# A transformer block with a mixture of experts on one core: routing's last steps, the pads, and the first expert pairs in another order

## The chip, the cores and the metric

The kernel runs on one core of a Trainium2 chip. The time is the device time of the whole program in microseconds; the lower, the better. TensorE is called PE, VectorE DVE, ScalarE ACT, GpSimd POOL and SyncE SP, as in the profile.

## The reference, cut to what matters

```python
x = L0_attn_x                                  # (16, 256, 128): 16 batches of 256 tokens, width 128
x = x + attention(layernorm(x))                # softmax, 16 heads
x = x + recurrence(layernorm(x))               # gated recurrence over 32 steps, its output tanh(...)
x = x + linear_attention(layernorm(x))         # rope, elu + 1 features, 16 heads
x = x + experts(layernorm(x))

def experts(xt):                               # xt: 4096 tokens of 128
    probs = softmax(xt @ Wr + br)              # 16 experts
    w, idx = top_k(probs, 2);  w = w / sum(w)
    h = gelu(xt @ W1[e] + b1[e])               # 128 -> 256, of each expert
    o = h @ W2[e] + b2[e]                      # 256 -> 128
    return xt + sum over the two chosen e of w[e] * o[e]
```

All data are float32. The residual of the last line is over the normalized tokens. Of two experts with logits l0 >= l1 the weights are 1/(1 + exp(l1 - l0)) and exp(l1 - l0)/(1 + exp(l1 - l0)), so one difference and one exponential give both.

## The kernel before, in words

Three parts follow each other. The first (attention and the recurrence, until about 326 us) is not touched.

**Routing.** `linear_attention_and_routing` works through 16 batches of 256 tokens as a pipeline. Each engine has its own function `iteration(n, r)` that lists, in an order written out by hand, the steps of that engine; each step works on batch `b = n - lag` and is left out when `active(n, lag)` is false. The order of the lines is the order of the engine's queue; engines meet only at semaphores (`wait_ge`, `then_inc`). A batch passes through these steps:

- PE and ACT make the recurrence's output, DVE adds it to X (x2), and takes the statistics of the third layernorm (`stats3`, then `mv`). POOL raises the variances of layernorm 3 and 4 to the power -0.5 (`root_power`, two instructions), DVE refines them in four small steps (`root_step` 0 to 3).
- ACT normalizes (`xn3`), PE turns it, makes q, k, v. DVE applies the rotation: t1, two products into t2 (lines 1211 and 1274), and their sum `rot` (line 1137, 128 x 512 with both inputs in SBUF). ACT copies V into `KVones`, makes the exponential and the relu, DVE joins them to `feat`.
- PE, ACT and DVE make the linear attention with its denominator (`KVm`, `den`, `on3`), and DVE adds the result to X (x3, line 1173) and takes `stats4`.
- ACT writes the normalized tokens twice into `pay`, PE makes the logits, ACT copies them. DVE finds the two best (`max`, `max_index`), marks them (`hot`, `sel`), PE counts how many tokens of each expert stand before each token, and DVE makes the place (`place`, `nup`, `mine`, line 1141, `pos`, line 1156). For the weights POOL takes the difference of the two best logits (`gap`, line 1067), ACT its exponential (`odds`, line 1298), DVE `z`, its reciprocal and the weights in `pay`.
- POOL scatters the rows of `pay` to `disp` in DRAM by `pos`: four indirect DMAs a batch (line 1035: two halves of the batch, two choices). Each expert has a region of 4096 + 128 rows there. POOL also adds the token to X (the residual, line 1074) and raises the row numbers in `pay` (the ids, line 1080).

POOL's order in an iteration is: second scatter of the last batch, root, third scatter, gap, fourth scatter, residual, ids, and the first scatter of the next.

**Routing's end.** `plan_tiles` on DVE turns the 16 counts in 17 dependent small steps into a table of 80 tiles of 128 rows (`tablei`): the expert of each tile, and its place in `disp`. `fill_pads` writes 128 empty rows behind the last row of each expert, so that the last tile of an expert reads zeros; SP does it for experts 0 to 7, ACT for 8 to 15. For each it loads the end from `endi` and issues one DMA. It starts after the plan's first step (`endi`).

**Experts.** The 80 tiles are worked on in 40 pairs. SP first waits for the scatters, the weights, the table and all pads, and then issues for each pair one word's load and two DMAs of 128 rows. PE turns the rows (`p_x`), ACT copies them (`xT`), PE multiplies with W1 (eight matmul instructions into `p_hid`), ACT does gelu (four instructions), PE multiplies with W2 (`p_y`), DVE scales by the weight and POOL scatters the rows to `back` (line 1576, two indirect DMAs a pair, 80 in all). DVE copies the weights of each pair's experts ahead (line 1628). In a step PE works on pair i (turn), i-1 (hidden) and i-2 (outputs), in that order; ACT first copies pair i, then does the gelu of pair i-1. At the end SP reads `back`, DVE adds it to X, and SP writes the output.

The lines that the argument about SP rests on are these:

```python
for e in range(q * E // 2, (q + 1) * E // 2):
    end = eng.value_load(endi[0:1, e:e + 1], min_val=e * REGION, max_val=e * REGION + TOKENS)
    eng.dma_start(disp[bass.ds(end, P), :], w["fill"][:, :]).then_inc(pads[q].sem, 16)
...
sp.wait_ge(table.sem, 1)
for q in range(2):
    sp.wait_ge(pads[q].sem, pads[q].at(0))
```

## Time and profile before

| what | us |
|---|---|
| median of three runs | 645.11 (643.07 to 648.98) |
| the profiled execution | 644.1 |
| its span | 642.3 |
| routing's even part in the span | 371.18 to 468.68 |
| first and last scatter of the experts, start | 517.80, 620.83 |

| engine | busy us | share of the span | instructions |
|---|---|---|---|
| PE | 486.8 | 76% | 4082 |
| DVE | 429.6 | 67% | 1260 |
| POOL | 388.7 | 61% | 691 |
| ACT | 341.4 | 53% | 733 |

The shares are means over stages with different limits, so none of them says what bounds the time. The profile follows the chain that ended last back from the end; in the span's last quarter it runs over POOL's scatters to `back`, before them over SP's queue with the pads, and before these over DVE and POOL of the routing. All times in this document that are positions are microseconds from the span's start.

### The profile page before, as it was taken

To read this page: it belongs to the slowest core of one execution; us is meant where nothing else is said; L and a number is where in the kernel's file an instruction comes from. 1 tells how busy PE (TensorE), PEld (TensorE's weight loads), DVE (VectorE), ACT (ScalarE), POOL (GpSimd) and SP (SyncE) were. 2 spreads that over 40 slices of the span, in tenths; PEclk is the share of its full clock that TensorE was granted. 3 is DMA by queue.
4 is the path that set the end of the run, shared out by engine and by line. 5 is a ranking of instruction groups with operands and counts; after the bars stand their busy time and mean duration, and the time that the engine had idled before them with its cause. 6 is when DMAs were issued, how large, how long until landed. Compare 5 with 4: busy or idle time off the path is not lost. (4 is left out here: it accounts for less than half of the span.)

```text
span 642.3 us, 14722 instructions
## 1 busy us (share of the span) xinstructions
PE 486.8 (76%) x4082; PEld 323.2 (50%) x4082; DVE 429.6 (67%) x1260; ACT 341.4 (53%) x733; POOL 388.7 (61%) x691
## 2 busy tenths in 40 slices
PE   1368899999999999988667887776861199899900
PEld 0123455555555555544434565454541199888800
DVE  6376778888888888852238889888866356555306
ACT  2016667777777777667215666655532076565600
POOL 4564587777777776332341477777777057777750
PEclk9999999999999999999859989999755599999955
DMA  2577444443443343200053000010012333333219
GB/s 65 139 181 188 105 101 122 101 103 103 101 100 101 98 109 102 55 4 2 0 168 101 13 31 31 30 35 30 31 35 65 71 98 95 97 95 100 77 53 350
DMA packets 66417, 55.97 MB, mean 87 GB/s; under 512 B 8477, under 2 KB 59826, under 8 KB 66354
## 3 DMA queue, kind: packets, MB, share of 16 engines
q1 hardware_dynamic: 58466, 45.12, 27.0%
q0 software_dynamic: 4608, 8.47, 4.0%
q10 hardware_dynamic: 3280, 1.65, 1.0%
q8 instruction: 27, 0.44, 0.3%
q14 instruction: 36, 0.29, 0.2%
HBM read 30.53 MB, written 25.71 MB: 88 GB/s over the span
## 5 line engine op out<-in xcount | busy, mean ns | idle before, releaser
L419 DVE TENSOR_REDUCE negmax<-p_dve 128x4 f32<-128x1024 f32 x128 | 155.8, 1220 | 44.3 <-PE p_dve L622 42.5
L518 ACT ACTIVATE probs<-p_exp 128x1024 f32<-128x1024 f32 x128 | 130.7, 1021 | 31.2 <-PE p_exp L596 30.7
L1576 POOL DMA_INDIRECT back<-XN2T,rows x80 | 79.9, 999 | 43.2 <-DVE XN2T L1636 21.9
L1035 POOL DMA_INDIRECT disp<-pay,pos x64 | 65.4, 1021 | 31.2 <-DVE pos L1156 19.4
L613 PE MATMUL p_out<-probs,V 128*32 128x256 f32 x1024 | 69.9, 391 | 0.0
L622 PE MATMUL p_dve<-KS,QS 61*128 61x256 bf16 x512 | 52.9, 289 | 13.6 <-DVE negmax L419 12.0
L1662 ACT ACTIVATE hid<-p_qkv,own 128x128 f32<-128x128 f32 x160 | 45.6, 368 | 24.6 <-PE p_qkv L1689 20.3
L596 PE MATMUL p_exp<-QS,KS 64*128 64x256 bf16 x512 | 51.0, 278 | 8.5 <-ACT probs L518 4.5
L1689 PE MATMUL p_qkv<-XN2T,own 128*128 128x128 f32 x320 | 44.2, 282 | 0.0
L1628 DVE COPY own<-expert 128x514 f32 x80 | 35.6, 446 | 12.7 <-issue 12.7
L1689 PEld LDWEIGHTS p_qkv<-XN2T,own 128*128 128x128 f32 x320 | 39.9, 196 | 0.9
L613 PEld LDWEIGHTS p_out<-probs,V 128*32 128x32 f32 x1024 | 27.1, 110 | 25.3 <-issue 14.3
L67 POOL TENSOR_SCALAR root<-mv 128x2 f32<-128x2 f32 x32 | 7.1, 221 | 51.4 <-DVE mv L411 50.2
L622 PEld LDWEIGHTS p_dve<-KS,QS 61*128 61x128 bf16 x512 | 22.8, 98 | 28.6 <-DVE negmax L419 23.9
L596 PEld LDWEIGHTS p_exp<-QS,KS 64*128 64x128 bf16 x512 | 14.7, 94 | 35.6 <-issue 15.5
L651 PE MATMUL p_misc<-ident,xn 128*128 128x128 f32 x64 | 15.2, 323 | 21.0 <-POOL xn L325 20.4
L570 ACT ACTIVATE gate<-p_misc,gates_bh 128x256 f32<-128x256 f32 x32 | 13.4, 470 | 23.1 <-PE p_misc L718 23.1
L69 POOL TENSOR_TENSOR root<-root,power 128x2 f32<-128x2 f32 x32 | 22.9, 717 | 2.7
L651 PEld LDWEIGHTS p_misc<-ident,xn 128*128 128x128 f32 x64 | 6.9, 150 | 34.4 <-POOL xn L325 19.2
L323 POOL TENSOR_TENSOR xn<-X,mv 128x256 f32<-128x256 f32 x32 | 19.6, 613 | 5.2 <-POOL root L78 2.1
L717 PE MATMUL p_misc<-xn2T,gates_w 128*128 128x256 f32 x64 | 20.8, 407 | 2.4 <-DVE carry L431 0.8
L675 PE MATMUL p_misc<-xn1T,Wqk 128*128 128x256 f32 x64 | 21.9, 473 | 1.0 <-ACT xn1T L529 0.9
(246 smaller groups left out, 1224.8 us busy)
## 6 DMA issues: line engine op xcount, KB each, us to landing
scratch<-part SPq DMA_DIRECT2D x32, 192.0 KB, 2.1
KS<-scratch SPq DMA_DIRECT2D x32, 192.0 KB, 3.3
QS<-scratch SPq DMA_DIRECT2D x32, 192.0 KB, 4.4
rows<-disp SPq DMA_DIRECT2D x80, 65.0 KB
scratch<-part SPq DMA_DIRECT2D x32, 128.0 KB, 1.9
own<-back SPq DMA_DIRECT2D x8, 512.0 KB, 6.4
expert<-in_W_dram SPq DMA_DIRECT2D x1, 2064.0 KB, 8.9
scratch<-part SPq DMA_DIRECT2D x32, 64.0 KB, 1.9
```

The source lines that it names most:

```text
L69: pool.tensor_tensor(y, v, t["power"][:, 0:TT], ALU.pow).then_inc(mark.sem, 1)
L419: dve.tensor_reduce(negmax[q][:, i, :, 2 * hp:2 * hp + 2], p_dve[buf][:, :].rearrange("p (v w k) -> p v w k", v=HALF, k=S), AX.X, ALU.max, ...
L518: act.activation(probs[s % 4][:, :, :, :].rearrange("p v w q -> p (v w q)"), p_exp[:, :], ACT.Exp)\
L596: mm = pe.matmul(p_exp[:, (2 * v + w) * S:(2 * v + w + 1) * S], KS[q][rows, h, kt * P:(kt + 1) * P], QS[q][rows, h, :], start=True, stop=True)
L613: mm = pe.matmul(p_out[32 * j:32 * j + 32, 0:S], values[:, first:first + 32], probs[s % 4][:, j % HALF, j // HALF, :], start=(s % 4 == 0), ...
L622: mm = pe.matmul(p_dve[buf][:, (2 * v + w) * S:(2 * v + w + 1) * S], QS[q][rows, h, i * P:(i + 1) * P], KS[q][rows, h, :], start=True, sto ...
L651: mm = pe.transpose(dst[:, i * P:(i + 1) * P], src[:, i, :], ident[:, :])
L1035: pool.indirect_dma_start(out=disp, out_offset=bass.IndirectOffsetOnAxis(ap=pos[q][:, i, k:k + 1], axis=0), in_=pay[q][:, k, i, :], in_off ...
L1576: pool.indirect_dma_start(out=back, out_offset=bass.IndirectOffsetOnAxis(ap=rows[r][:, h, D + 1:ROW].bitcast(U32), axis=0), in_=y[r][:, h, :],
L1628: dve.tensor_copy(own[r][:, h, :], w["expert"][:, bass.ds(es[h], 1), :].rearrange("p o c -> p (o c)")).then_inc(w_s.sem, 1)
L1662: act.activation(hid[q][:, h, c, :], p_hid[q % 2][:, (2 * h + c) * P:(2 * h + c + 1) * P], ACT.Gelu, bias=own[q][:, h, HID + c:HID + c + 1 ...
L1689: mm = pe.matmul(p_hid[q % 2][:, (2 * h + c) * P:(2 * h + c + 1) * P], own[q][:, h, c * P:(c + 1) * P], xT[q][:, h * P:(h + 1) * P], start ...
```

## The change

**Two pad ends in a word.** The counts, without the region's start, are packed in pairs, the second shifted by 13 bits, with three more plan steps for one less (17 become 19). SP takes the pairs of experts 0-1, 4-5, 8-9, 12-13, ACT the others; each loads four words instead of eight and issues eight DMAs as before. The pads start after the plan's fourth step. **A tile for every expert:** an expert without rows gets one tile (the clamp to P). **First pads with their own signal:** the pads of experts 0 to 3 count on `pads_first`; SP waits for these before it starts, and for the other twelve only before pair 2.

```diff
-            then(dve.tensor_copy(endi[:, :], count[:, :]))
+            then(dve.tensor_tensor(full[:, :], count[:, :], w["region"][:, :], ALU.subtract))
+            then(dve.tensor_copy(endi[:, :], full[:, :]))
+            ends = endi[:, :].rearrange("p (j k) -> p j k", k=2)
+            then(dve.tensor_scalar(ends[:, :, 1], ends[:, :, 1], END_BITS, None, ALU.logical_shift_left))
+            then(dve.tensor_tensor(ends[:, :, 0], ends[:, :, 0], ends[:, :, 1], ALU.bitwise_or))
...
-            then(dve.tensor_tensor(full[:, :], count[:, :], w["region"][:, :], ALU.subtract))
-            then(dve.tensor_scalar(counti[:, :], full[:, :], float(P - 1), None, ALU.add))
+            then(dve.tensor_scalar(counti[:, :], full[:, :], float(P - 1), float(P), ALU.add, ALU.max))
...
-            eng.wait_ge(plan.sem, plan.at(0, 1))
+            eng.wait_ge(plan.sem, plan.at(0, 4))
             eng.wait_ge(fill_set.sem, fill_set.at(0))
-            for e in range(q * E // 2, (q + 1) * E // 2):
-                end = eng.value_load(endi[0:1, e:e + 1], min_val=e * REGION, max_val=e * REGION + TOKENS)
-                eng.dma_start(disp[bass.ds(end, P), :], w["fill"][:, :]).then_inc(pads[q].sem, 16)
+            for pair in range(q, E // 2, 2):
+                word = eng.value_load(endi[0:1, 2 * pair:2 * pair + 1], min_val=0, max_val=(TOKENS << END_BITS) + TOKENS)
+                for k in range(2):
+                    rows = nc.s_assert_within((word >> END_BITS * k) & ((1 << END_BITS) - 1), 0, TOKENS,
...
+                    place = rows + (2 * pair + k) * REGION
+                    eng.dma_start(disp[bass.ds(place, P), :], w["fill"][:, :])\
+                        .then_inc(pads_first.sem if pair < FIRST_PADS // 2 else pads[q].sem, 16)
...
+        sp.wait_ge(pads_first.sem, pads_first.at(0))
         sp.wait_ge(table.sem, 1)
-        for q in range(2):
-            sp.wait_ge(pads[q].sem, pads[q].at(0))
...
+            if isinstance(i, int) and 2 * i == FIRST_PADS:
+                for q in range(2):
+                    sp.wait_ge(pads[q].sem, pads[q].at(0))
```

**The routing's order.** Blocks that stood at the start of DVE's, PE's and POOL's iteration stand at its end, with the lag lowered by one, so that the pipelines are one iteration shorter; ACT's logits copy goes the other way. Apart from this rotation, these instructions change places in their engine's cyclic order:

- DVE before: t1, x2, t2 (line 1211), KVm, root 0, 1, 2, max, root 3, max_index, den, hot, reciprocal, sel, z, on3, t2 (line 1274), place, reciprocal of z, nup, rot, mine, pay, pos, stats3, x3, feat, stats4.
- DVE after: x2, t1, t2, KVm, root 0, **second t2**, root 1, max, **root 2**, max_index, den, **root 3**, hot, reciprocal, sel, z, on3, **reciprocal of z**, place, **rot, nup, stats3**, mine, pay, pos, x3, feat, stats4.
- POOL before: first scatter, second, root, third, gap, fourth, residual of this batch, ids of the next. POOL after: residual of this batch, its ids, first scatter, root, second, third, fourth scatter; no gap.
- ACT: V's copy goes from behind on3T to between the logits' copy and the exponential.
- PE: only rotated.

**The logits' difference by ACT.** The exponential takes it as scale and bias, one instruction for each half of the batch:

```diff
-                    pool.tensor_tensor(gap[:, :], best[:, :, 1], best[:, :, 0], ALU.subtract).then_inc(gap_s.sem, 1)
...
-                    act.wait_ge(gap_s.sem, gap_s.at(b))
+                    act.wait_ge(top_s.sem, top_s.at(b, TT))
...
-                    act.activation(odds[:, 1, :], gap[:, :], ACT.Exp).then_inc(odds_s.sem, 1)
+                    for i in range(TT):
+                        act.activation(odds[:, 1, i:i + 1], best[:, i, 0:1], ACT.Exp, bias=best[:, i, 1:2], scale=-1.0).then_inc(odds_s.sem, 1)
```

**The first pairs.** With FILL = 3, PE and ACT do the older pairs first in the steps 0 to 3; from step 4 on the order is as before:

```diff
+        def step(i, k, r):
+            if isinstance(i, int) and i <= FILL:
+                hidden(i, k, r)
+                outputs(i, k, r)
+                turn(i, k, r)
+            else:
+                turn(i, k, r)
+                hidden(i, k, r)
+                outputs(i, k, r)
```

ACT likewise: `hidden` (gelu) and then `turned` (the copy) up to step 3, `turned` and then `hidden` after it.

## Rows read from the trace of the kernel before

**Rows 1.** Stage table, routing's even part: us, busy (instructions) of each engine, clock, DMA.

```profile
371.18:468.68 97.50, 74.09 (x430) 51.46 (x431) 85.49 (x413) 55.49 (x149) 75.20 (x99) 0.94 0.10 31
```

**Rows 2.** Timeline of POOL over one routing period: start us, duration us, engine, line, operation.

```profile
417.87 0.96 POOL L1035 DMA_INDIRECT disp<-pay,pos  x1 [0.30 <-DVE stats L1189]
...
419.18 1.04 POOL L1053 TENSOR_TENSOR root<-root,power 128x4 f32<-128x4 f32 x1
420.42 1.09 POOL L1035 DMA_INDIRECT disp<-pay,pos  x1 [0.20 <-issue]
421.54 0.21 POOL L1067 TENSOR_TENSOR gap<-best 128x2 f32<-128x2 f32 x1
421.90 0.99 POOL L1035 DMA_INDIRECT disp<-pay,pos  x1 [0.16 <-issue]
422.91 0.70 POOL L1074 TENSOR_TENSOR X<-X,pay 128x256 f32<-128x256 f32 x1
423.70 0.57 POOL L1080 TENSOR_SCALAR pay<-pay 128x4 int32<-128x4 int32 x1
425.37 1.07 POOL L1035 DMA_INDIRECT disp<-pay,pos  x1 [1.10 <-DVE pos L1156]
```

**Rows 3.** Timeline of DVE in the same period; brackets: idle before, and its releaser.

```profile
420.25 0.16 DVE L1104 TENSOR_TENSOR root<-root 128x4 f32<-128x4 f32 x1 [0.66 <-POOL root L1053]
...
423.00 1.17 DVE L1137 TENSOR_TENSOR rot<-t 128x512 f32<-128x512 f32 x1
...
424.34 0.22 DVE L1156 TENSOR_REDUCE pos<-mine 128x4 uint32<-128x64 f32 x1
424.48 0.48 DVE L1162 BATCH_NORM_STATS2 stats<-X 128x6 f32<-128x128 f32 x2
...
425.25 0.39 DVE L1173 TENSOR_TENSOR X<-p_u,X 128x256 f32<-128x256 f32 x1
```

**Rows 4.** One line's instructions (rot on DVE): duration ns min/median/max, first and last start.

```profile
L1137 DVE TENSOR_TENSOR rot<-t x16: 681/1171/1180, 338.8 to 467.3; 128x512 f32<-128x512 f32 x16
```

**Rows 5.** One line's instructions (the pads' DMAs on SP): duration ns, first and last start.

```profile
L958 SPq DMA_DIRECT2D disp<-fill x8: 332/332/372, 493.5 to 501.5; - x8
```

**Rows 6.** The chain of waits from the last pad to the first rows: start us, us.

```profile
501.51 4.14 DMA disp<-fill
...
506.62 0.37 SPq L1600
...
507.36 0.35 SPq L1600
...
508.56 0.34 SPq L1600
```

**Rows 7.** Timeline of PE and ACT at the first expert pairs.

```profile
509.31 0.66 PE L1679 MATMUL p_ta<-ident,rows 128*128 128x128 f32 x2 [12.98 <-DMA rows<-disp]
510.01 0.38 ACT L1654 ACTIVATE XN2T<-p_ta 128x256 f32<-128x256 f32 x1 [18.15 <-PE p_ta L1679]
...
512.04 1.91 PE L1689 MATMUL p_qkv<-XN2T,own 128*128 128x128 f32 x8
...
513.99 1.14 ACT L1662 ACTIVATE hid<-p_qkv,own 128x128 f32<-128x128 f32 x4 [1.32 <-PE p_qkv L1689]
514.17 1.18 PE L1689 MATMUL p_qkv<-XN2T,own 128*128 128x128 f32 x8
```

**Rows 8.** Timeline of POOL, first and last scatter of the expert stage.

```profile
517.80 1.01 POOL L1576 DMA_INDIRECT back<-XN2T,rows  x1 [19.12 <-DVE XN2T L1636]
...
620.83 0.97 POOL L1576 DMA_INDIRECT back<-XN2T,rows  x1 [0.30 <-issue]
```

**Rows 9.** Timeline of ACT in the same period.

```profile
421.77 0.20 ACT L1298 ACTIVATE odds<-gap 128x2 f32<-128x2 f32 x1 [2.27 <-POOL gap L1067]
```

**Rows 10.** Timeline of POOL near routing's end: first scatter right after the ids.

```profile
486.25 1.07 POOL L1035 DMA_INDIRECT disp<-pay,pos  x1 [0.78 <-POOL pay L1080]
```

**Rows 11.** Timeline of DVE in the tile plan, four steps merged.

```profile
493.38 0.81 DVE L927 TENSOR_TENSOR tiles<-tiles 128x16 f32<-128x16 f32 x4
```

More of the change, by code:

```diff
@@ new lines, in iteration @@
+                if active(n, 5):
+                    b = n - 5
+                    dve.wait_ge(pos_s.sem, pos_s.at(b, 3))
+                    if b >= PAIR:
+                        dve.wait_ge(sent[b % PAIR].sem, sent[b % PAIR].at(b // PAIR - 1))
+                    with nc.allow_low_precision(reason="one term of each sum is not zero, and it is a whole number"):
+                        dve.tensor_reduce(pos[o][:, :, :], mine[:, :, :, :], AX.X, ALU.add).then_inc(pos_s.sem, 1)
+                if active(n, 3):
+                    b = n - 3
+                    dve.wait_ge(u_p.sem, u_p.at(b))
+                    dve.wait_ge(nm3.sem, nm3.at(b))
+                    dve.tensor_tensor(X[:, bass.ds(2 * b, 2), :], p_u[:, 0:S].rearrange("p (i d) -> p i d", i=TT), X[:, bass.ds(2 * b, 2), :], ALU.add)\
+                        .then_inc(x3_s.sem, 1)
@@ L1286, in _ @@
+            pipeline(dve, iteration, 5)
             plan_tiles(dve)
@@ L1670, in expert_pe, with turn @@
         pe.wait_ge(table.sem, 1)
-        def step(i, k, r):
+        def turn(i, k, r):
             if i is not None:
```

296 lines of the change are left out of this document (146 added, 150 removed).

## The prediction

> **What bounds the kernel now.** I read the stage table first, then one period of the routing stage engine by engine, then the chain of waits from the last batch to the first expert pair, and last the scatters of the expert stage.
>
> In the routing stage each batch takes one period. The window of [rows 1] is 97.50 us long and holds 99 POOL instructions; a period has nine (four scatters, two of the root, gap, residual, ids), so these are eleven periods of 8.86 us. No engine is full: DVE is busy 85.49 of 97.50. What sets the period is a loop over two engines. DVE writes pos, which ends at 424.56; POOL starts the first scatter at 425.37, 0.8 us later, then comes a second, then the root ([rows 2] show the second scatter and the root of the period before, 417.87 to 420.22); DVE has nothing left to do for 0.66 us until the root is there ([rows 3]) and takes 4.31 us from it to the end of the next pos (420.25 to 424.56). POOL's part is 8.86 - 4.31 = 4.55 us. A second thing to see: POOL's residual (422.91, 0.70 us) and DVE's rot (423.00) overlap, and rot takes 1.17 us, where its shortest takes 0.681 ([rows 4]).
>
> Between the routing and the experts nobody computes. After the last pos SP and ACT issue eight pads each, 1.14 us apart ([rows 5]); SP waits 4.14 us for the last, and only then issues the first rows ([rows 6]). PE turns them at 509.31, and the first scatter of the experts starts at 517.80 ([rows 7, 8]). From there POOL issues 80 scatters without a hole to 620.83: 103.03 / 79 = 1.30 us each, 2.6 per pair of tiles. POOL bounds that stage, so the end of the kernel moves with the first of these scatters, 517.80, and with nothing else of the stage's middle.
>
> **The rotation costs nothing.** Most of the diff moves the blocks across the iteration's start with the lag lowered by one. The instructions of one engine then come in the same cyclic order, with the same waits; PE is only rotated. What is left are these real moves.
>
> **Routing, per period.** (a) POOL's second scatter (0.96 us, and 0.30 before it) goes behind the root. After the end of pos = 0: first scatter 0.8 to 1.9, root to 3.3 ([rows 2]: 418.83 to 420.22 is 1.39), and DVE goes on at 3.3, no longer at 4.55. (b) DVE's stats of X now stand before mine and pos: + 0.77 (424.48 to 425.25, [rows 3]) between root and pos. (c) The third rotation product is brought between the root's steps: the work is the same, it fills short gaps; I count 0, at most 0.2. (d) Gap leaves POOL: 0.21 and the slots around it, 421.51 to 421.90, are replaced by the 0.30 that stands between two scatters, so 0.1 us. ACT does two exps of 0.20 us for one, and the copy of V stands in front of them; it idles 2.27 us before the exp ([rows 9]), and V's copy is 0.38 (the same size as the one of [rows 7]). Cost 0; if that cover were gone, DVE's z would wait up to 0.4 us. (e) The residual and the ids stand ahead of the batch's own scatters instead of behind the last batch's: the same place in the cycle, right after a fourth scatter.
>
> If rot kept its 1.17 us the loop would be 3.3 + 4.31 + 0.77 = 8.4. But where does the residual fall now? POOL from pos = 0: root to 3.3, 0.20, scatter 1.09, 0.30, 0.96, 0.30, 0.96, so the residual runs from 7.1 to 7.8. Rot starts at 3.3 + 2.75 = 6.05 (420.25 to 423.00), ahead of it: 0.49 less. Mine comes 0.68 + 0.77 later, at 7.5, inside the residual: it pays instead, between 0 and 0.70, and I take rot's own 0.49. So the stall is handed on, not removed. The loop is 8.4 - 0.49 + 0.49 = 8.4 with both, 7.9 with neither. Followed from the residual's end instead, mine, pay and pos need some 0.4 more, which gives 7.8 + 0.4 = 8.2; I take that.
>
> The next bound stands close behind: POOL's own queue. 1.07, 1.39, 0.20, 1.09, 0.30, 0.96, 0.30, 0.96, 0.03, 0.70, 0.09, ids 0.23 to 0.57, and 0.78 from ids to the next scatter ([rows 10]) give 8.1 to 8.4. So the new period is 8.2, with bounds 8.0 and 8.5: 0.66 us less than 8.86. I count 12 periods (eleven of the window and one for the uneven ones at its ends): 7.9 us. Once, the first batch's pos comes 0.77 later behind the stats: less 0.8. In the tail the root can stand in POOL's queue waiting for its stats with a scatter behind it; nothing to at most 0.7, I take 0.1. Routing: **-7.0 us**, bounds -3.5 and -9.5.
>
> The Trainium skill, SBUF: State Buffer, section Who interferes with whom, says that a DVE instruction with two SBUF inputs and a GpSimd instruction that reads SBUF lock each other out for the whole instruction, whoever starts first. By that rule rot and mine each wait for the residual's end; the trace agrees for rot, which ends 0.56 us after the residual does.
>
> **From the last pos to the first expert scatter.** Two more plan steps and the pads four steps in instead of one: a step is 0.2 us (0.81 for four, [rows 11]), so the pads start 0.6 later, at 494.1 instead of 493.5. The table is 0.4 later and waits for nobody: 17 + 2 steps of 0.2 and the short ones behind them are done while the pads go out. A word now gives two DMAs. The rows' loads of SP already do this: 506.62, 507.36, 508.56, that is 1.94 a word and 0.74 inside ([rows 6]). Eight pads: 3 x 1.94 + 0.74 = 6.56 instead of 7.98, the last at 500.7 instead of 501.5. SP then no longer waits 4.14, since its remaining waits are over: the first pads went out 6 us earlier, and POOL's last scatter ends 0.8 + 1.07 + 3 x 1.26 = 5.7 after pos and has 4 us more to land, as long as a pad takes. About 0.5 for the issue and the waits, 0.97 from there to the first row DMA (505.65 to 506.62): 502.2, the second 502.9, and PE at + 1.95 (507.36 to 509.31) = 504.9: 4.4 us earlier. The other end: if the reads stand behind the pads in the DMA engines, they start when the last has landed, 500.7 + 4.14 + 1.95 = 506.8, and 2.5 is left. I take 4.2. The wait for all pads before pair 2 ends at 504.9 at the latest, when pair 1 has just been issued: 0. The clamp to one tile an expert adds no instruction, and all 80 tiles were run before.
>
> **Order of the first pairs.** With T = PE's first turn: turn 0.66, copy 0.38, hidden 0 from T+1.15, at 1.91 (the slow clock) to T+3.1 ([rows 7]). Then ACT does the four gelus first (1.14) and the copy of pair 1 behind them, so hidden 1 starts at T+4.65; before it started at T+4.86. From there to the first scatter 3.63 (514.17 to 517.80). That is 0.2 won. But until pair 4 each pair now goes hidden 1.06 to 1.18, gelus 1.14, copy 0.38, with hand-overs about 2.9 us in series, where POOL takes 2.6: it starves 0.3 for each of two or three pairs. And PE, which went from 1.91 to 1.18 for the eight hidden matmuls while it was busy without a hole from 512.04, has a hole of 0.9 us after turn 1; if its clock stays at 1.2 GHz for one or two pairs more, each costs 0.75 and the outputs as much. Bounds: -0.2 and +2.8; I take **+1.1**, between. So the hand-over gains 4.2 - 1.1 = **3.1 us**.
>
> **The sum** is 7.0 + 3.1 = 10.1 us. Against the profiled execution, 644.1 (span 642.3 and 1.8 around it), that is 634.0; its time is 1.0 under the median of the three runs, 645.11, which gives 635.0. I write 634.5, between the two.
>
> **Rivals.** (1) Rot on a scatter, the slower case. Rot now starts at 6.05, where POOL's third scatter (4.9 to 5.85) ends and the fourth begins (6.15). If a scatter shuts out a DVE instruction with two SBUF inputs as the residual does, rot waits for 7.1, and if POOL's residual slips in ahead of it, for 7.8; rot, stats, mine and pos then end at 7.8 + 0.68 + 0.77 + 0.5 = 9.75. Twelve periods of + 0.9 are + 10.8, less the 3.1 gained: 653. It turns slower from a period of 9.1 on. Against it: from 420.42 to 422.89 POOL is in a scatter nearly all the time, and DVE gets through its stretch from root to rot without a hole in it. Chance 0.05. (2) Something else closes the routing loop: rot waits only for the scatter, or DVE for ACT's exps, and the period stays near 8.8. Left are 3.1 and a little: 641. For it: three engines hang on each other within 0.3 us here. 0.18. (3) The first pads' own signal does not do what it says: the reads stand behind the pads and PE starts cold, so the hand-over gains 0 to 1: 637.5. 0.12. (4) Better than forecast: neither rot nor mine meets the residual and POOL's slots close up, period 8.0, and no starving: 630. 0.15.
>
> **Chances.** The forecast (period 8.1 to 8.35 and 2 to 4 us at the hand-over, 632 to 637) has 0.50. A measurement can tell about 1% (6.5 us) from no change: faster means under 638.7. The forecast, case 4 and most of case 3 lie there, with a part of case 2: 0.76; within 1%: 0.19; slower 0.05. The range that leaves out two in ten takes in cases 4 and 2: 629 to 642.
>
> **What will show it.** Routing: first scatters 8.2 us apart (8.87 now); DVE's wait for the root under 0.3; rot at 0.68 and mine at about 0.7; the ACT row before the exp still idle. Hand-over: last pad on SP 6.6 us after the first instead of 8.0; first rows without the 4.14 us wait; PE's first turn 10.8 us after the first pad instead of 15.8; first expert scatter about 9 us after the turn instead of 8.5. From there to the end 124.5 us as before. If the period is over 8.6 the POOL and lock arithmetic is wrong; if the turn comes over 12.5 us after the first pad, the reads queue behind the pads.

## The result and the profile after

| | before, us | after, us |
|---|---|---|
| median of 20 runs each, in turn on one chip | 645.22 (641.59 to 651.56) | 642.75 (636.30 to 650.22) |
| the profiled execution, its span | 644.1, 642.3 | 639.8, 638.0 |

The ratio after to before is 0.9919, 95% interval 0.9893 to 0.9945: 5.2 us faster. It leaves out the slow runs, which are over 1.5% above their kernel's fastest (five of after's 20 and one of before's), while the medians in the table hold all of them and are 2.5 us apart. The forecast was a gain of 10.6. 642.75 lies outside the range of 629 to 642, and nearest to rival 2's 641.

I cut both traces at the same five events: the first scatter of routing's first and of its last batch, PE's first turn of an expert pair, POOL's first expert scatter and its last.

| stretch, us | before | after | change | forecast |
|---|---|---|---|---|
| start to the first batch's scatter | 363.13 | 360.23 | -2.9 | 0 |
| first to last batch | 129.99 | 122.69 | -7.3 | -7.0 |
| last batch to PE's turn | 16.19 | 13.01 | -3.2 | -4.2 |
| turn to the first expert scatter | 8.49 | 10.24 | +1.7 | +1.1 with the next |
| first to last expert scatter | 103.03 | 108.82 | +5.8 | 0 |
| last expert scatter to the end | 21.47 | 23.01 | +1.5 | 0 |

The first row is not the change's: that part of the kernel is the same, and in 19 traces of the two kernels and their variants it was between 359.8 and 368.5, on average 363.1 with the old routing and 362.9 with the new. So this one pair of profiles flatters the change by 3 us there, and the two last rows take 7.3 away.

**Routing.** The stage table of after, over twelve periods from the third batch to the fifteenth (columns as in [rows 1]), has 97 POOL instructions in 99.11 us, eight a period instead of nine, and 8.26 us a period:

```profile
376.53:475.64 99.11, 74.50 (x428) 52.02 (x428) 83.76 (x421) 59.60 (x159) 77.01 (x97) 0.86 0.10 34
```

The timeline of POOL in one period of after (against [rows 2]):

```profile
389.99 0.96 POOL L1046 DMA_INDIRECT disp<-pay,pos  x1 [0.30 <-issue]
390.98 0.69 POOL L1072 TENSOR_TENSOR X<-X,pay 128x256 f32<-128x256 f32 x1
391.76 0.23 POOL L1078 TENSOR_SCALAR pay<-pay 128x4 int32<-128x4 int32 x1
392.76 1.07 POOL L1046 DMA_INDIRECT disp<-pay,pos  x1 [0.77 <-POOL pay L1078]
393.86 0.24 POOL L1062 TENSOR_SCALAR root<-mv 128x4 f32<-128x4 f32 x1
394.18 1.04 POOL L1064 TENSOR_TENSOR root<-root,power 128x4 f32<-128x4 f32 x1
```

The period is 8.12 here, and what stands before the first scatter is no longer DVE's pos but POOL's own ids, as in [rows 10]: in an undisturbed period POOL's queue is the bound. The timelines of DVE and ACT of the same period (against [rows 3, 4, 9]):

```profile
387.13 0.16 DVE L1109 TENSOR_TENSOR root<-root 128x4 f32<-128x4 f32 x1 [0.27 <-POOL root L1064]
...
389.37 0.68 DVE L1228 TENSOR_TENSOR rot<-t 128x512 f32<-128x512 f32 x1
...
390.83 0.27 DVE L1246 TENSOR_TENSOR mine<-hot,place 128x64 f32<-128x64 f32 x1
391.02 0.68 DVE L1253 TENSOR_TENSOR pay<-odds,z 128x4 f32<-128x4 f32 x1
391.62 0.21 DVE L1261 TENSOR_REDUCE pos<-mine 128x4 uint32<-128x64 f32 x1
```

```profile
387.71 0.39 ACT L1312 ACTIVATE KVones<-p_qkv 128x256 f32<-128x256 f32 x1 [0.53 <-DVE t L1158]
387.99 0.47 ACT L1320 ACTIVATE odds<-best 128x1 f32<-128x1 f32 x2
```

DVE's wait for the root is 0.27 (0.66 before), rot takes 0.68, and the residual (390.98 to 391.67) is paid for by the instruction behind mine, the weights in `pay`: 0.68 us for an operation on 128 x 4 that usually took 0.15 in before, ending as the residual ends. The stall was handed on, to a neighbour of the one I named. ACT's 2.27 us of idleness before the exp, which I expected to stay, are gone, filled by V's copy and the second exp, and DVE's z waits for neither.

**The hand-over.** SP's pads, the chain from the last scatter, and the landing time of routing's scatters in a usual period (the last column):

```profile
484.03 6.58 SPq L968 DMA_DIRECT2D disp<-fill  x8
```

```profile
485.55 0.96 POOL disp L1046
486.51 0.30 issue
486.81 5.71 DMA disp<-pay,pos
492.60 0.27 SPq L1601
...
493.36 0.37 SPq L1608
494.08 1.71 DMA rows<-disp
```

```profile
disp<-pay,pos POOLq DMA_INDIRECT x4, 2.3
```

The eight pads take 6.58 us for the forecast 6.56. The chain no longer has a pad in it: it runs over the last scatter's landing, which takes 5.71 us from the scatter's start, where 2.3 is usual in the routing. But the last scatter of before, which also runs beside the 16 pads, is late too:

```profile
disp<-pay,pos POOLq DMA_INDIRECT x1, 5.0
```

It landed at 502.0, hidden behind the last pad, which landed at 505.65 ([rows 6]). In e1 to e7 the last landing takes 4.4 to 5.1 us. So the change didn't bring the late landing, it uncovered it.

**The first pairs.** PE and ACT (against [rows 7]):

```profile
495.93 0.66 PE L1697 MATMUL p_ta<-ident,rows 128*128 128x128 f32 x2 [9.32 <-DMA rows<-disp]
497.06 2.07 PE L1709 MATMUL p_qkv<-XN2T,own 128*128 128x128 f32 x8 [0.47 <-ACT XN2T L1662]
499.17 1.14 ACT L1672 ACTIVATE hid<-p_qkv,own 128x128 f32<-128x128 f32 x4 [2.16 <-PE p_qkv L1709]
...
500.64 2.07 PE L1709 MATMUL p_qkv<-XN2T,own 128*128 128x128 f32 x8 [1.08 <-ACT XN2T L1662]
...
505.75 2.07 PE L1709 MATMUL p_qkv<-XN2T,own 128*128 128x128 f32 x8 [0.47 <-ACT XN2T L1662]
...
510.41 1.16 PE L1709 MATMUL p_qkv<-XN2T,own 128*128 128x128 f32 x8 [0.26 <-ACT XN2T L1662]
```

Three pairs' hidden matmuls take 2.07, where before only the first was slow (1.91). PE stands before each of them, and its granted clock stays at 1.2 GHz until 509.3, for 13.4 us after the first turn; before it was 5.1. And POOL:

```profile
511.00 0.98 POOL L1582 DMA_INDIRECT back<-XN2T,rows  x1 [2.54 <-DVE XN2T L1644]
...
513.96 0.98 POOL L1582 DMA_INDIRECT back<-XN2T,rows  x1 [0.70 <-issue]
```

It starves 2.24 and 0.40 us beyond its usual 0.30.

**The middle of the experts.** The expert scatters of before and of after, each as a row of the lines by form (busy us, mean ns, idle us before them):

```profile
L1576 POOL DMA_INDIRECT back<-XN2T,rows x80 | 79.9, 999 | 43.2 <-DVE XN2T L1636 21.9 <-issue 21.3
```

```profile
L1582 POOL DMA_INDIRECT back<-XN2T,rows x80 | 83.1, 1039 | 45.1 <-DVE XN2T L1644 23.1 <-issue 22.0
```

The same 80 scatters take 3.2 us more, and that is all of the difference from the fifth to the last (97.85 and 101.03 us). Three of before are over 1.2 us, 14 of after; over 1.1 us are 7 and 19. Most others are at 0.97 or 0.98. DVE, then POOL, around two of the long ones of after:

```profile
517.50 0.51 DVE L1636 COPY own<-expert 128x514 f32 x1
...
518.03 0.41 DVE L1636 COPY own<-expert 128x514 f32 x1
```

```profile
516.52 1.23 POOL L1582 DMA_INDIRECT back<-XN2T,rows  x1 [0.30 <-issue]
518.06 1.23 POOL L1582 DMA_INDIRECT back<-XN2T,rows  x1 [0.30 <-issue]
```

A copy of an expert's weights (518.03) starts 0.03 before the scatter (518.06) and ends 0.38 into it; all 14 of over 1.2 us look so. The copy before it, which began while a scatter ran, is itself 0.51 instead of 0.42. The same trace holds a test of whether any DVE instruction would do this, an addition with one input in PSUM, and a hit by a copy that is nearer its end:

```profile
533.21 0.42 DVE L1644 TENSOR_TENSOR XN2T<-p_r,rows 128x256 f32<-128x256 f32 x1 [1.20 <-PE p_r L1724]
533.26 0.98 POOL L1582 DMA_INDIRECT back<-XN2T,rows  x1 [0.30 <-issue]
...
571.14 0.43 DVE L1636 COPY own<-expert 128x514 f32 x1 [0.52 <-issue]
571.33 1.09 POOL L1582 DMA_INDIRECT back<-XN2T,rows  x1 [0.30 <-issue]
```

The addition stands as the copy does, and the scatter stays at 0.98. The copy at 571.14 has 0.24 us left when the scatter starts, and costs 0.11. Over all nine traces with plain copies the same sum holds: where a copy began over 0.03 us before a scatter and had over 0.13 us left, in 147 cases, the scatter is longer by what was left of the copy less 0.13 us, to within 0.06; the additions that stood across a start, 89 of them, left it at 1.03 or less. The Trainium skill (SBUF — State Buffer, section Who interferes with whom) says that a copy in its fast mode and GpSimd block each other for a whole instruction, and that writing the descriptors of a GpSimd DMA needs the shared port. The traces agree, and price it: up to 0.25 us a hit.

### The profile page after: what moved, and what is told of

Same layout as the page of the kernel before. It is cut to its first block and busy times, and to the rows that moved or that the text cites. A ratio compares the mean times of both kernels' runs of the same rounds, so it can differ in the third digit from the quotient of the medians.

```text
span 638.0 us, 14709 instructions
## 1 busy us (share of the span) xinstructions
PE 487.8 (76%) x4082; PEld 324.2 (51%) x4082; DVE 428.4 (67%) x1262; ACT 348.1 (55%) x749; POOL 386.5 (61%) x675
## 5 line engine op out<-in xcount | busy, mean ns | idle before, releaser
L1582 POOL DMA_INDIRECT back<-XN2T,rows x80 | 83.1, 1039 | 45.1 <-DVE XN2T L1644 23.1
L1046 POOL DMA_INDIRECT disp<-pay,pos x64 | 66.1, 1032 | 30.8 <-issue 13.1
L613 PE MATMUL p_out<-probs,V 128*32 128x256 f32 x1024 | 68.5, 385 | 0.0
L1709 PE MATMUL p_qkv<-XN2T,own 128*128 128x128 f32 x320 | 46.6, 291 | 2.3 <-ACT XN2T L1662 2.3
L1709 PEld LDWEIGHTS p_qkv<-XN2T,own 128*128 128x128 f32 x320 | 41.2, 202 | 4.8 <-ACT XN2T L1662 3.7
L596 PEld LDWEIGHTS p_exp<-QS,KS 64*128 64x128 bf16 x512 | 14.7, 94 | 35.5 <-issue 15.5
L570 ACT ACTIVATE gate<-p_misc,gates_bh 128x256 f32<-128x256 f32 x32 | 13.4, 471 | 23.3 <-PE p_misc L718 23.3
L1363 ACT ACTIVATE pay<-X,root 128x256 f32<-128x256 f32 x32 | 17.4, 593 | 14.2 <-issue 12.0
```

Of the source, the lines that this page charges most:

```text
L596: mm = pe.matmul(p_exp[:, (2 * v + w) * S:(2 * v + w + 1) * S], KS[q][rows, h, kt * P:(kt + 1) * P], QS[q][rows, h, :], start=True, stop=True)
L613: mm = pe.matmul(p_out[32 * j:32 * j + 32, 0:S], values[:, first:first + 32], probs[s % 4][:, j % HALF, j // HALF, :], start=(s % 4 == 0), ...
L1046: pool.indirect_dma_start(out=disp, out_offset=bass.IndirectOffsetOnAxis(ap=pos[q][:, i, k:k + 1], axis=0), in_=pay[q][:, k, i, :], in_off ...
L1582: pool.indirect_dma_start(out=back, out_offset=bass.IndirectOffsetOnAxis(ap=rows[r][:, h, D + 1:ROW].bitcast(U32), axis=0), in_=y[r][:, h, :],
L1709: mm = pe.matmul(p_hid[q % 2][:, (2 * h + c) * P:(2 * h + c + 1) * P], own[q][:, h, c * P:(c + 1) * P], xT[q][:, h * P:(h + 1) * P], start ...
```

## The experiments

The theory after the first look: routing pays as forecast, the hand-over pays less because of the last scatter's landing, and the rest is lost at two places where the forecast saw none: the order of the first pairs under the slow clock, and copies that lengthen the scatters of a stage bound by POOL. The rival: the order is harmless and the whole shortfall lies in the routing, or comes with the pads. Every kernel was run in five rounds in turn with the kernel before, six or twelve times. All times below are from profiled executions; "fifth to last" is from POOL's fifth expert scatter to its last.

| kernel | ratio to before (95%) | routing, first to last batch | last batch to turn | turn to fifth scatter | fifth to last | scatters busy |
|---|---|---|---|---|---|---|
| before | 1 | 129.99 | 16.19 | 13.67 | 97.85 | 79.9 |
| after | 0.9919 (0.9893, 0.9945) | 122.69 | 13.01 | 18.03 | 101.03 | 83.1 |
| e1, old order of pairs | 0.9892 (0.9831, 0.9953) | 123.02 | 12.55 | 14.37 | 100.21 | 82.3 |
| e2, only the order | 1.0015 (0.9970, 1.0060) | 129.94 | 15.95 | 16.04 | 98.09 | 80.1 |
| e3, only routing | 0.9905 (0.9865, 0.9946) | 125.69 | 15.60 | 15.43 | 99.86 | 82.0 |
| e4, only routing's end | 0.9965 (0.9925, 1.0005) | 130.64 | 12.90 | 13.49 | 99.22 | 81.2 |
| e5, extra matmuls | 0.9870 (0.9807, 0.9933) | 127.75 | 13.14 | 13.05 | 100.79 | 82.9 |
| e6, the same, old order | 0.9876 (0.9817, 0.9936) | 125.22 | 13.79 | 12.22 | 99.81 | 81.8 |
| e7, copies with two inputs | 0.9956 (0.9916, 0.9995) | 123.35 | 13.12 | 16.34 | 104.48 | 87.1 |

**e1, the old order of the first pairs.**

```diff
-FILL = 3
+FILL = -1
```

> The changed kernel with one part undone: PE and ACT work on the first pairs in the old order (turn, hidden, outputs; copy, gelu). Theory A (the new order leaves PE in holes behind ACT, its clock stays at 1.2 GHz, and POOL starves): the fifth expert scatter starts about 13.7 us after PE's first turn, as before the change, instead of 18.0, and the time falls by about 4 us against the changed kernel, ratio to the kernel before 0.983 to 0.988. Theory B (the expert stage lost its time to DVE's weight copies and POOL's scatters shutting each other out, whatever the order): the fifth scatter may come earlier, but the number of scatters over 1.2 us stays near 20 and the time falls by at most 1 us, ratio about 0.991. Theory C (the gain of the routing is not real in most runs): about 1.00.

Turn to fifth scatter falls from 18.03 to 14.37 us, without a hole before any scatter. PE's timeline of e1, the first three pairs:

```profile
500.13 1.91 PE L1709 MATMUL p_qkv<-XN2T,own 128*128 128x128 f32 x8
...
502.26 1.91 PE L1709 MATMUL p_qkv<-XN2T,own 128*128 128x128 f32 x8
...
506.02 1.06 PE L1709 MATMUL p_qkv<-XN2T,own 128*128 128x128 f32 x8
```

PE runs on without a hole from its second turn, and the clock is up 7.4 us after the first. This is theory A's time to the fifth scatter; the gain by the ratio, 0.9892, is a little smaller than it said (0.983 to 0.988), and its interval covers that of after. Ten scatters are over 1.2 us.

**e2, before with the new order alone** (`step` of PE and ACT as in the change, FILL = 3; nothing else).

```diff
+            if isinstance(i, int) and i <= FILL:
+                hidden(i, k, r)
+                outputs(i, k, r)
+                turn(i, k, r)
```

> The kernel before with the new order of the first pairs alone. Theory A: fifth expert scatter 17 to 18 us after PE's first turn instead of 13.7, 4 us slower, ratio 1.006. Theory B: the first scatter moves by under 2 us and the time by nothing that can be told, unless the scatters over 1.2 us become many more than 5; ratio 0.998 to 1.003.

2.4 us more to the fifth scatter than before (16.04, 13.67), less than theory A's 17 to 18, and a ratio above 1 that can't be told from it. The order costs, with either hand-over.

**e3, before with the routing's part alone**: the moved steps and the difference by ACT; the pads, the plan and the order are those of before.

```diff
-                    act.activation(odds[:, 1, :], gap[:, :], ACT.Exp).then_inc(odds_s.sem, 1)
+                    for i in range(TT):
+                        act.activation(odds[:, 1, i:i + 1], best[:, i, 0:1], ACT.Exp, bias=best[:, i, 1:2], scale=-1.0).then_inc(odds_s.sem, 1)
```

> The kernel before with the routing's part alone (orders of DVE, POOL, ACT and PE, the exponential of the logits' difference by ACT); plan, pads and the order of the first pairs are the old ones. Routing gains what its trace shows: the last batch's first scatter 10 us earlier, hand-over 24.7 us as before, expert stage 103 us. All theories but C: 635, ratio 0.984 to 0.987. Theory C: 0.995 or above. Theory B leaves open 0 to 4 us of longer scatters by chance of phase.

6.1 us by the ratio, with 2.6 either way: the change's gain and perhaps more, but not the 8 to 10 that was expected. The trace has 125.69 us from the first to the last batch, 3 more than after: most periods are 8.1, but four are 8.9 to 9.6. POOL's timeline at one of them, where the first scatter comes 9.60 us after the last batch's:

```profile
408.23 1.06 POOL L1035 DMA_INDIRECT disp<-pay,pos  x1 [1.93 <-ACT pay L1352]
```

This trace also shows that the old order alone doesn't bring the fifth scatter at 13.7. Its clock comes up 8.6 us after the turn, as in e2 with the new order, and its fifth scatter 15.43 us after it. In the eight traces with the old order and no extra matmuls the clock is up 5.1 to 8.6 us after the turn, in the seven with the new 8.6 to 13.4. On the later chips the fifth scatter comes after 15.5 to 16.6 us with the old order and 17.2 to 17.7 with the new.

**e4, before with routing's end alone** (plan, pads, signal; routing and order of before).

```diff
+        sp.wait_ge(pads_first.sem, pads_first.at(0))
         sp.wait_ge(table.sem, 1)
-        for q in range(2):
-            sp.wait_ge(pads[q].sem, pads[q].at(0))
```

> The kernel before with the end's part alone (two pad ends per word, first pads with their own signal, one tile for every expert), old routing order and old order of the first pairs. PE's first turn 3 us earlier after the last batch's first scatter, 13.0 instead of 16.2; the last scatter of the routing lands in about 5.7 us instead of 2.3, which now ends SP's wait. Theories A and B: 642, ratio 0.993 to 0.997. If the pads were hidden behind something else: 1.00.

The turn comes 12.90 us after the last batch's first scatter instead of 16.19, and the fifth scatter 3.5 us earlier; the ratio gives 2.3 us. The last landing takes 4.76 us here, not the 5.7 that I expected. Routing and hand-over together are worth 8.4 by the ratios of e3 and e4, the order costs 1.0 by that of e2: 7.4, where after measures 5.2 with an interval of 3.5 to 6.9. Each of the three is uncertain by 2.6 to 2.9 us, so the two sums can't be told apart.

**e5 and e6, extra matmuls before the first pair**, to raise the clock; e5 with the new order, e6 with the old (FILL = -1). Nothing reads their product.

```diff
         pe.wait_ge(table.sem, 1)
+        for _ in range(13):
+            pe.matmul(p_hid[1][:, 0:256], ident[:, :], w["expert"][:, 0, 0:256], start=True, stop=True)
```

> The changed kernel with 13 extra matmuls of 128x256 on PE (their result is overwritten) in the 8 us in which PE waits for the first rows. If the slow clock is what makes the new order dear, the first hidden matmuls take 1.1 us instead of 2.07, the fifth expert scatter comes 15 us after the first turn instead of 18.0, and about 3 us are gained. If the serial order itself costs it, the clock is at 2.4 GHz and the fifth scatter still comes after 17 us or more. Theory B (shut-outs between DVE's copies and POOL's scatters): nothing from the fifth scatter to the last changes, 99 to 101 us.

> The same extra matmuls, and the old order of the first pairs. The difference to the kernel with the new order and the same clock is the order's own price: theory A says 1.5 to 2 us at the fifth scatter (12.5 to 13 us after the turn). Time about 634, ratio 0.982. Theory B: from the fifth scatter to the last as with the new order.

PE of e5, the first two pairs:

```profile
503.18 1.16 PE L1711 MATMUL p_qkv<-XN2T,own 128*128 128x128 f32 x8 [0.47 <-ACT XN2T L1662]
...
505.84 1.16 PE L1711 MATMUL p_qkv<-XN2T,own 128*128 128x128 f32 x8 [1.06 <-ACT XN2T L1662]
```

The clock is at 2.4 GHz from 4.6 and 2.8 us before the turn. There the new order needs 13.05 us to the fifth scatter and the old 12.22. So the order's own price is 0.8 us (1.5 to 2 was expected), by one trace of each (0.6 by e2 and e3, whose clocks come up together); the rest of its 2.4 us (e2 against before) to 3.7 us (after against e1) is the clock that it keeps down. Both kernels have the lowest ratios of all, and cannot be told apart by them.

**e7 and e8, the weight copies as an instruction with two inputs** (x * 0 + x, both from SBUF), to take them out of the fast mode; e8 with the old order and the extra matmuls. The small copy of b2 is changed likewise, here and in the later kernels.

```diff
-                    dve.tensor_copy(own[r][:, h, :], w["expert"][:, bass.ds(es[h], 1), :].rearrange("p o c -> p (o c)")).then_inc(w_s.sem, 1)
+                    one = w["expert"][:, bass.ds(es[h], 1), :].rearrange("p o c -> p (o c)")
+                    dve.scalar_tensor_tensor(out=own[r][:, h, :], in0=one, scalar=0.0, in1=one, op0=ALU.mult, op1=ALU.add).then_inc(w_s.sem, 1)
```

> The changed kernel, but DVE copies the experts' weights with a two-operand instruction (x * 0 + x, both operands the same tile) instead of its copy. Theory B: such an instruction does not keep POOL from writing descriptors, so no scatter of the expert stage is over 1.2 us, their busy time is 78 instead of 83.1, the stretch from the fifth scatter to the last is 96.3 us instead of 101.0, and the time falls by 4 us or more, ratio 0.984 to 0.987. Theory A: the weight copies are longer and nothing is gained; ratio 0.991 or more.

> All three together: old order of the first pairs, extra matmuls before them, weight copies with two operands. If theories A and B are both right, fifth scatter 13 us after the turn and 96.3 us from it to the last: 9 us less than the changed kernel in the expert stage, about 632, ratio 0.977 to 0.981. If one of them is wrong, that part's 4 us are missing.

The opposite of what I expected. DVE, then POOL, of e7:

```profile
517.11 0.69 DVE L1637 SCALAR_TENSOR_TENSOR own<-expert 128x514 f32 x1
```

```profile
517.21 1.44 POOL L1582 DMA_INDIRECT back<-XN2T,rows  x1 [0.48 <-issue]
```

The scatter that starts under the longer instruction takes 1.44 us, the stage 104.5 instead of 101.0. The instruction had 0.59 us left, so the copy's sum (less 0.13) gives 1.44 here too: this instruction with two inputs in SBUF holds a scatter back as the copy does, and longer because it is longer. In the nine traces of before, after and e1 to e7 the stretch from the fifth scatter to the last is the scatters' busy time and 17.3 to 18.0 us more, so a longer scatter lengthens the stage by as much. e8's ratio is 0.9897 (0.9857, 0.9936), 0.2% above its sister e6, where 0.977 to 0.981 was expected; its profile isn't read.

**e9, e10, e11: the copies as a reduce over one element**, which the Trainium skill's same section lists as never contending on trn2. e9 is after, e10 before, e11 after with the old order and the extra matmuls.

```diff
-                    dve.tensor_copy(own[r][:, h, :], w["expert"][:, bass.ds(es[h], 1), :].rearrange("p o c -> p (o c)")).then_inc(w_s.sem, 1)
+                    one = w["expert"][:, bass.ds(es[h], 1), :].rearrange("p o c -> p c o")
+                    dve.tensor_reduce(own[r][:, h, :], one, AX.X, ALU.max).then_inc(w_s.sem, 1)
```

> The changed kernel with DVE's weight copies as a reduction over an axis of one element (max): one operand in SBUF, about 0.6 us for 514 elements instead of 0.43. The kernel with two operands made the shut-outs worse (scatters up to 1.4 us, 104.5 us from the fifth to the last), so theory B now reads: any DVE instruction that reads SBUF through a second port holds POOL back, the longer the more, and one with a single plain operand does not. It expects all scatters at 0.97 to 1.0, busy time 78, 96 to 97 us from the fifth to the last, 4 us less than the changed kernel, ratio 0.984 to 0.988. The rival: any longer DVE instruction at a scatter's start delays it, and this one does as well: 103 us or more. The Trainium skill, SBUF: State Buffer, Who interferes with whom, says of tensor_reduce on this chip that it never contends.

> The kernel before with the same weight copies. Theory B: the kernel before had few shut-outs (97.9 us from the fifth scatter to the last), so it gains 1.5 us at most, ratio 0.996 to 1.000; with the changed kernel and the same copies beside it the whole of the change then shows, 8 to 9 us. The rival: 103 us, slower by 5.

> The changed kernel with the reduction as copy, the old order of the first pairs and the 13 extra matmuls before them: fifth scatter 12.5 us after the turn, 96 to 97 us from there to the last. Theories A and B together: 9 to 10 us under the changed kernel's expert stage, time about 633, ratio 0.976 to 0.982, under both kernels. If the reduction does not free POOL: 0.985 to 0.99, as with the old order alone.

No scatter is long any more; its row of one line in e9 (ns min/median/max):

```profile
L1582 POOL DMA_INDIRECT back<-XN2T,rows x80: 978/982/997, 511.6 to 648.1; - x80
```

and in e12, DVE's reduce starts 0.10 us before a scatter and has 0.59 left at its start, as the instruction of e7 had, with no effect:

```profile
519.57 0.69 DVE L1637 TENSOR_REDUCE own<-expert 128x514 f32 x1
519.67 0.98 POOL L1582 DMA_INDIRECT back<-XN2T,rows  x1 [0.30 <-DVE XN2T L1646]
```

But the times don't price it. On this chip the kernel before took 678.5 us, and the expert stage of all three kernels has 35 to 36 us of holes before POOL's scatters, 15 or 16 of about 2.2 us and some smaller ones, where before's own trace has none; at more than half of them PE, DVE and ACT have stood together shortly before, for 0.9 to 2.8 us. The ratios are 0.9888 (0.9850, 0.9926), 1.0007 (0.9979, 1.0036) and 0.9906 (0.9872, 0.9940).

**e12 to e17, the same kernels on other chips.** e12 and e16 are e9, e13 and e17 are e10, e14 is e11; e15 is after with reduces and FILL = -1, without the extra matmuls.

> The kernel after with the experts' weight copies done by a reduce over one element, once more, because the chip of the last comparison showed holes of 35 us in the expert stage, in which POOL is not the bound and a longer scatter costs nothing. Theory (copies lengthen the scatters, which bound the stage on an undisturbed chip): no scatter over 1.2 us, and fifth to last scatter 97.5 to 98.5 us where the changed kernel had 101.0; the whole time 2 to 3.5 us under the changed kernel's, a ratio to the kernel before of 0.985 to 0.989. Rival (the longer scatters are filled from slack elsewhere): 101 us again, with holes before the scatters, and a ratio of 0.992.

> The kernel before with the same copies by reduce. Theory: the profiled run of the kernel before had only 2 long scatters and 97.9 us from the fifth to the last, so a profile hardly changes (97.5 to 98.5), but its usual run is likely to have more of them (variants had 7 to 18), so the median falls by 0 to 2 us: ratio 0.997 to 1.000. Rival: ratio 1.000 or above, as the longer DVE instruction (0.69 us for 0.42) costs what the scatters win.

> The kernel after with copies by reduce, the old order of the first pairs and extra matmuls before the first pair. Theory: routing -7.3, hand-over -2.5 to -4, expert stage 97.5 to 98.5: the whole 9 to 11 us under the kernel before, ratio 0.983 to 0.986, the forecast's size. Rival (the longer scatters cost nothing): as its sister with plain copies, 0.9876.

> The kernel after with copies by reduce and the old order of the first pairs, nothing else. Theory, on a chip whose expert stage has no holes: fifth to last scatter 97.5 to 98.5 us, turn to fifth scatter 13.5 to 14.5: 9 to 11 us under the kernel before, ratio 0.983 to 0.986. Rival (longer scatters cost nothing): as the old order with plain copies, 0.9892. On a chip with holes: 0.989 either way.

> The kernel after with copies by reduce, in case this chip has no holes in the expert stage. Theory: 97.5 to 98.5 us from fifth to last scatter, ratio 0.985 to 0.989. Rival: 100 to 101 us and 0.992.

> The kernel before with copies by reduce, in case this chip has no holes in the expert stage. Theory: 97.5 to 98.5 us, ratio 0.997 to 1.000. Rival: 1.000 or above.

| kernel | ratio to before (95%) | before there, us | fifth to last | longest scatter |
|---|---|---|---|---|
| e12 | 0.9921 (0.9878, 0.9964) | 677.5 | 129.83 | 1.00 |
| e13 | 0.9982 (0.9947, 1.0016) | 677.5 | 128.53 | 1.01 |
| e14 | 0.9893 (0.9857, 0.9930) | 677.5 | 129.96 | 1.00 |
| e15 | 0.9884 (0.9845, 0.9923) | 675.6 | 127.11 | 1.00 |
| e16 | 0.9946 (0.9907, 0.9986) | 675.6 | 126.60 | 1.00 |
| e17 | 1.0056 (1.0021, 1.0091) | 675.6 | 128.72 | 1.01 |

The holes again, so no price again. Nine traces of 80 scatters, and not one over 1.01 us.

**e18, the changed kernel unaltered**, on such a chip.

> The changed kernel unaltered, as the control for the nine runs with reduces: in their calls the kernel before took 675 to 678 us, and the reduces' traces have 16 holes of about 2.2 us before POOL's scatters in the expert stage. If the holes are the chip's, this trace has them too (33 to 36 us), with scatters over 1.2 us beside them, and the ratio is 0.989 to 0.993. If they are the reduces', this trace has under 4 us of holes, and the kernel before takes 643 to 648 us.

The ratio is 0.9933 (0.9894, 0.9971), before took 675.9, and the trace has 31 us of holes: they belong to the chips, not to the reduce. POOL's timeline shows one, and a lengthened scatter:

```profile
560.58 0.98 POOL L1582 DMA_INDIRECT back<-XN2T,rows  x1 [2.23 <-DVE XN2T L1644]
...
563.28 1.07 POOL L1582 DMA_INDIRECT back<-XN2T,rows  x1 [0.42 <-issue]
```

With copies, five scatters are over 1.1 us here (19 in after's first trace). What holds the engines up on these chips stays open.

**What the traces show together.** From the first to the last batch, the six traces with the old routing took 129.9 to 131.0 us. The thirteen with the new took 122.7 to 130.0, on average 125.7. The profile of after is the best of the thirteen. The periods say how: from the second batch to the thirteenth they are 8.81 to 8.90 with the old routing, in all six traces, but for the last one in two of them (9.18 and 9.28). With the new they start at 8.08, and in each trace some are held up: one of the eleven is over 8.6 us in after, three in e3, e5 and e6 each, six in e11, the longest 10.53.

What holds them up is a wait that neither the prediction nor the words ahead of it name. ACT writes a batch's tokens into one of two buffers `pay`, and must first wait until the scatters of the batch two before have landed:

```python
if b >= PAIR:
    act.wait_ge(sent[b % PAIR].sem, sent[b % PAIR].at(b // PAIR - 1))
```

One of the longest periods, in e5: the landing time of the scatter at 366.91 (the last of its batch), then ACT and POOL,

```profile
disp<-pay,pos POOLq DMA_INDIRECT x1, 4.2
```

```profile
371.14 1.09 ACT L1363 ACTIVATE pay<-X,root 128x256 f32<-128x256 f32 x2 [2.58 <-issue]
...
379.69 1.15 POOL L1046 DMA_INDIRECT disp<-pay,pos  x1 [2.83 <-ACT pay L1363]
```

The scatter lands at 371.06 and ACT goes on at 371.14; the profile calls the wait "issue", but the landing is what ends it. In the traces that record these landings (not all do), ACT starts `pay` within 0.1 us of one in 49 of 61 batches with the new routing, and in 3 of 33 with the old, where 1.0 us of slack is usual. A landing mostly takes 2.3 us from the scatter's start. With the old routing five took over 3 us (up to 4.34), and the periods behind them are 8.81 to 8.88. With the new nine did: one of 3.23 in after costs nothing (8.15), and behind the other eight stand periods of 8.87 to 10.53. Five periods of over 8.6 in these traces (8.80 to 9.16) come without a late landing. Why some scatters land late isn't known.

The slow clock may add to it. In e3 it is at 1.2 GHz from 402.5 to 405.9, inside the period of 9.60. In e5 it falls only at 378.2, when most of the delay is there. The kernel before takes both at once without a loss. There a scatter lands after 3.54 us, and the clock is slow from 371.1 to 374.5; stage table of 3 us,

```profile
371.00:374.00 3.00, 3.00 (x8) 1.62 (x7) 2.60 (x15) 2.24 (x4) 1.49 (x2) 0.51 0.09 26
```

and the next first scatter comes 8.81 us after the last, as always. How much of a long period is the landing's and how much the clock's, no run separates.

## Why the prediction was wrong, step by step

**The routing's bound: right, its size right only undisturbed.** The loop over DVE and POOL, the root's wait, rot at 0.68, a stall that is handed on and POOL's queue close behind all stand in the trace. POOL's queue gives 8.11, the lower end of 8.1 to 8.4. But I read the regularity of the old period as a property of the work. It was that of its slack: the buffer wait for the landings stands in both kernels, I put it at nothing without looking, and the shorter period uses up the 1.0 us of slack that hid it. The typical gain is 4.6 us over all traces (130.3 to 125.7), and 5.6 (130.2 to 124.6) over those of ordinary chips (where before takes 645 to 648 us), not 7.0; the bounds of -3.5 to -9.5 hold both.

**The hand-over's start: right mechanism, 1.0 us too much.** The pads are as forecast. Their signal works: the turn comes 11.9 us after the first pad, where I forecast 10.8 and named 12.5 as the sign that the reads queue behind the pads. What is off is SP's last wait, which I called over. Pos ended at 492.31 in before, so my own terms (5.7 to the scatter's end, 4 more to land) put the landing at 502.0, and SP was to be through at 501.2: 0.8 us that I dropped. The landing itself came 4.75 us after the scatter's end instead of 4, another 0.75; 0.5 came back in smaller terms. That the pads in flight make it late is likely, since it is 2.3 from the start in the routing, against 5.0 to 5.7 here; no run took the pads away. In this trace the first reads are as quick beside the pads as without them, 2.57 us from the first row DMA to the turn for 2.69 before. In e1, e4, e5, e6 and e7 the landing is earlier and the reads take 3.3 to 4.4, so there they seem to be held up in part, and over all traces the hand-over's start gains 2.7 us (15.8 to 13.1).

**The order of the first pairs: its own price right, its clock not.** 0.8 us at the full clock for the forecast +1.1, which was to include the clock, and 2.4 to 3.7 at the slow one. The bound of +2.8 was built from two slow pairs; in after three stayed slow, each with its outputs, the longest of all traces.

**"POOL bounds that stage, so the end of the kernel moves with the first of these scatters, 517.80, and with nothing else of the stage's middle": this is the step that failed.** From there to the end I forecast 124.5 us; it took 131.8. 2.6 are the starving behind the new order, which I had priced before the first scatter and where I had written off what follows. 3.2 are scatters lengthened by DVE's copies: e7 makes them longer, the reduces remove them, and the length follows what is left of the copy, so the cause is shown; what removing them is worth in time is not, since all reduce runs fell on chips where POOL isn't the bound. 1.5 are in the output stage of this one profile; the other traces on ordinary chips have 21.4 to 22.2, so I count it as chance.

Whether the change itself causes more hits stays open. The three traces with the old routing and plain copies (before, e2, e4) have 97.9 to 99.2 us from the fifth to the last scatter and 7 to 13 scatters over 1.1 us; the five with the new (after, e1, e3, e5, e6) have 99.8 to 101.0 and 12 to 19. A copy hits when it starts between 0.03 and 0.3 us before a scatter, and each trace is one draw of how they fall.

With the typical values the sum comes near the measured one: routing -5.6, hand-over -2.7 (15.8 to 13.1 on average), order +2.6 (14.2 to 16.8 to the fifth scatter), expert stage +2 at most: -3.7 to -5.7, against -5.2 (-3.5 to -6.9). The forecast had -10.1 for the four. Of what is missing by these values, 1.4 us come between the first expert scatter and the fifth and up to 2 behind it, 1.5 in the hand-over and 1.4 in the routing: the failed step is the largest part, and not the only one. Of the rivals none was right as written. Rival 2's number was nearest, but its mechanism, a loop that stays at 8.8, shows only in single periods.

## What to carry to other kernels

A period that is the same in every trace to 0.1 us may have slack in it, and a bound worked out from instruction times is its best case: price what a slow clock or a late engine costs once the slack is gone. A wait that costs nothing in the trace before may be the next bound, so go through the waits that the code has and not only through those that the trace shows, the ones for a free buffer above all. A queue that is full to the end bounds a stage, but its instructions have no fixed length: before an edit moves another engine's copies against it, look at the spread of its longest ones. And an order that puts a waiting engine first in the cold steps pays twice, once for the hand-over and once for the clock that it keeps down.

## What was not expected of the hardware

- An indirect scatter by POOL is lengthened by what DVE runs at its start: by what is left of a one-input fp32 copy less 0.13 us, from 0.98 to 1.23 us at the usual place; to 1.44 and at most 1.49 by a two-input instruction (0.69 us long, 0.58 to 0.63 left); not at all by a reduce of the same 128 x 514 (0.68 us), nor by an addition with one input in PSUM (0.42 us).
- Routing's scatters land 2.3 us after their start, but single ones take 3.0 to 4.3, and the last one, beside 16 pads of 128 rows, 4.4 to 5.7.
- The kernel before took 645 to 648 us in the first three comparisons and 675 to 678 in the four later ones, on four other chips, with 13 to 17 pauses of POOL of about 2 us in the expert stage of every kernel profiled there. The change's ratio is the same on both within its interval (0.9919 and 0.9933).
